# Attention between two routed FFNs on one core: score banks in pairs, three query tiles moved by squares, values later

## The reference, cut to what matters

```
q = LN(x) @ Wq.T + bq
scores = q @ memory_keys.T / sqrt(128)          # 4096 tokens x 4096 keys
probs = softmax(scores)
x = x + (probs @ memory_values) @ Wo.T + bo
```

## Time and profile before

| | us |
|---|---|
| time, median of 3 runs | 713.45 (712.92 to 713.6) |
| the profiled execution: its time | 712.66 |
| its span | 710.6 |
| TensorE busy | 644.7 |
| VectorE busy | 533.0 |
| ScalarE busy | 470.7 |
| GpSimd busy | 285.5 |
| mean granted TensorE clock (share of 2.4 GHz, no time) | 0.99 |

### The profile page before, as it was taken

The page is one execution under the profiler, slowest core; times in us unless marked ns, Lnnn a source line. Parts: engine busy times, 40 slices in busy tenths (PEclk is TensorE's granted clock), DMA queues, the critical chain, the costliest instruction groups (busy, mean ns, idle before and its releaser), DMA issues.

```text
span 710.6 us, 9499 instructions
## 1 busy us (share of the span) xinstructions
PE 644.7 (91%) x3009; PEld 453.5 (64%) x3024; DVE 533.0 (75%) x1048; ACT 470.7 (66%) x893; POOL 285.5 (40%) x354
## 2 busy tenths in 40 slices
PE   3898988769999999999999999999999989889997
PEld 2444443557777777777777776777777777645542
DVE  3799876757867787677686877767777885799885
ACT  3577887546675665766766667666666556478886
POOL 4655412043534434254252443425433547642200
PEclk9899999989999999999999999999999999999999
DMA  7011100225043150422505224051340504000001
GB/s 280 2 37 54 59 30 0 65 55 119 15 104 81 40 119 8 112 66 55 119 1 118 57 63 104 15 119 36 85 107 13 119 9 110 1 0 31 30 15 45
DMA packets 24803, 44.39 MB, mean 62 GB/s; under 512 B 4955, under 2 KB 5555, under 8 KB 24627
## 3 DMA queue, kind: packets, MB, share of 16 engines
q1 hardware_dynamic: 24467, 43.78, 24.6%
q10 hardware_dynamic: 288, 0.01, 0.0%
HBM read 8.12 MB, written 2.10 MB: 14 GB/s over the span
## 4 chain that ended last, share of the span: by engine, by line
PE 40%; DVE 31%; ACT 15%; issue 9%; POOL 2%; SPq 1%; DMA 1%; ACTq 0%; DVEq 0%; POOLq 0%
DVE bank_max L929 10%; DVE E L881 8%; DVE p_lo L874 5%; ACT E L629 4%; PE banks L1175 4%; ACT probs L639 4%; PE banks L1055 4%; PE banks L1220 4%; PE banks L1222 3%; PE banks L1221 3%; PE banks L1064 3%; PE banks L1177 3%; PE banks L1176 3%; ACT p_hi L606 3%; DVE probsT L788 3%
## 5 line engine op out<-in xcount | busy, mean ns | idle before, releaser
L418 POOL TENSOR_TENSOR p_lo<-probsT,p_hi 128x512 fp32r<-128x512 f32 x128 | 164.3, 1289 | 286.6 <-ACT p_hi L614 286.6
L929 DVE TENSOR_REDUCE bank_max<-banks 128x1 f32<-128x512 f32 (+1 forms) x192 | 162.0, 853 | 23.4 <-PE banks L1177 21.0
L874 DVE TENSOR_TENSOR p_lo<-banks,p_hi 128x512 fp32r<-128x512 f32 x128 | 87.7, 685 | 97.0 <-ACT p_hi L606 96.8
L629 ACT ACTIVATE E<-banks,neg_max 128x512 f32<-128x512 f32 (+1 forms) x96 | 79.3, 830 | 91.8 <-DVE neg_max L954 86.2
L1175 PE MATMUL banks<-kv_lo,q_parts 128*128 128x512 f32 x256 | 113.9, 445 | 27.0 <-ACT probs L639 13.4
L639 ACT ACTIVATE probs<-banks,neg_max 128x512 f32<-128x512 f32 (+1 forms) x96 | 79.3, 830 | 73.3 <-DVE neg_max L954 73.3
L509 ACT ACTIVATE probsT<-probsT 128x1024 bf16<-128x1024 bf16 x96 | 92.3, 981 | 33.0 <-DVE probsT L788 24.3
L788 DVE SCALAR_TENSOR_TENSOR probsT<-banks,E 128x1024 bf16<-128x1024 f32 x80 | 95.5, 1219 | 22.5 <-PE banks L1055 19.6
L1220 PE MATMUL banks<-p_hi,kv_lo 128*128 128x512 f32 x256 | 107.9, 421 | 1.5 <-POOL p_lo L418 1.3
L1222 PE MATMUL banks<-p_hi,kv_hi 128*128 128x512 f32 x256 | 102.3, 400 | 0.0
L1221 PE MATMUL banks<-p_lo,kv_hi 128*128 128x512 f32 x256 | 102.0, 399 | 0.0
(11 more groups left out here) (101 smaller groups left out, 867.7 us busy)
## 6 DMA issues: line engine op xcount, KB each, us to landing
probsT<-E SPq DMA_DIRECT2D x256, 128.0 KB, 2.4
kv_stage<-in_keys_values SPq DMA_DIRECT2D x8, 512.0 KB, 3.5
out<-X SPq DMA_DIRECT2D x8, 256.0 KB, 2.0
X<-in_x SPq DMA_DIRECT2D x1, 1280.0 KB, 9.2
X<-in_x SPq DMA_DIRECT2D x3, 256.0 KB, 5.3
probs<-in_wup SPq DMA_DIRECT2D x1, 704.0 KB, 5.3
probs<-in_wdown SPq DMA_DIRECT2D x1, 704.0 KB, 6.6
sup_s<-in_shared_up SPq DMA_DIRECT2D x1, 88.0 KB
```

Of the source, the lines that this page charges most:

```text
L418: pool.tensor_tensor(moved_part(p_lo, ring), moved_pair(w, m), moved_part(p_hi, ring).bitcast(fp32), ALU.subtract).then_inc(moved_lo_done, 1)
L874: dve.tensor_tensor(own_part(p_lo, ring), own_squares(ring), own_part(p_hi, ring).bitcast(fp32), ALU.subtract).then_inc(p_lo_done, 1)
L929: dve.tensor_reduce(bank_max[:, i % 2, k:k + 1], score_banks(u, i)[:, first:first + count, :].rearrange("p b n -> p (b n)"), AX.X, ALU.max ...
```

## The change: pairs of banks, a third moved tile, a later value sum

1. **Banks.** Banks 0 to 5 are three pairs (SCORE_PAIRS). Half a tile's scores (two banks, 1024 keys) fill one pair. The programs walk over **half tiles**, 8 a unit, counted through as H = 8u + h. The scores of half H wait for the exponential of half H - 3. There is one bank TB (bank 6) for all transposes and projections, and one bank OB (bank 7) for the value sums.
2. **Tiles.** MOVED = 3: tiles 0 to 2 go by squares, TensorE transposes only tile 3 (two transposes for each pair of chunks). The transfers go in two batches of 16: tiles 0 and 1 after their squares, then tile 2 after its own.
3. **Lag.** In half H TensorE transposes pair H - 12 (FILL_HALF) and sums the values of pair H - 14 (VALUE_HALF).
4. **Maxima and exponentials** are 1024 wide throughout (before: 1024, 512, 512 and 512, 512, 1024).
5. **Blocks.** Each unit's projection goes to TB, ScalarE copies it to y for both blocks, and GpSimd multiplies it by the share and adds it to X (`add_block`); VectorE no longer does it.
6. Buffers share other memory: kv_stage lies in E2's third tile, the xT copies in probs, the staged FFN weights in probsT.

The diff, cut to its core:

```diff
-EXP_PIECES = ((0, 1), (1, 1), (2, 2))
-MOVED = 2
+MOVED = 3
+OWN = GT - MOVED
+BATCHES = ((0, 2), (2, 1))
-VLAG = 4
-MAX_BANKS = ((0, 2), (2, 1), (3, 1))
+SCORE_PAIRS = 3
+HALVES = 2 * GT
+LAG = 12
+FILL_HALF = HALVES + LAG // 2 - 2
+VALUE_HALF = HALVES + LAG // 2
+PROJECT_HALF = LAG // 2 + 1
+Q_HALF = 5
...
+        def score_pair(u, i, h):
+            p = (2 * (u * GT + i) + h) % SCORE_PAIRS
+            return banks[:, 2 * p:2 * p + 2, :]
...
+        def pair_at(H, first_half):
+            return H - first_half if 0 <= H - first_half < UNITS * UP else None
...
         # sync
-                sp.wait_ge(squares_done, 2 * MOVED * (u + 1))
-                for b in range(QUADS):
-                    for i in range(QUADS):
-                        sp.dma_start(
+                for k, (first, count) in enumerate(BATCHES):
+                    sp.wait_ge(squares_done, 2 * (MOVED * u + first + count))
+                    for b in range(QUADS):
+                        for i in range(QUADS):
...
+                            sp.dma_start(target, E2[i * SQ:(i + 1) * SQ, first:first + count, b, :]
+                                         ).then_inc(moved[k], 16)
...
         # gpsimd
+            def add_block(w):
+                g, v = w // 2, w % 2
+                pool.wait_ge(y_copied, w + 1)
+                pool.wait_ge(merge_b, 4 * g + 4)
+                pool.tensor_tensor(y[:, :, :], y[:, :, :], share[:, v, :].unsqueeze(2).to_broadcast([P, GT, D]),
+                                   ALU.mult).then_inc(y_scaled, 1)
...
+                pool.tensor_tensor(X[:, tiles_of(g), :], X[:, tiles_of(g), :], y[:, :, :], ALU.add
+                                   ).then_inc(block_added, 1)
...
+                    ring = pair_at(u * HALVES + h, VALUE_HALF - 4)
+                    if ring is not None:
+                        moved_low(ring)
...
+                    if 2 <= u and h == LAG // 2:
+                        add_block(u - 2)
...
         # scalar, in each half
+                    if 2 <= u and h == LAG // 2 - 2:
+                        copy_oT(u - 2)
+                    ring = pair_at(H + 1, FILL_HALF)
+                    if ring is not None:
+                        own_high(ring)
+                    if u < UNITS:
+                        exponentials(u, h // 2, h % 2)
...
+                    ring = pair_at(H, VALUE_HALF - 4)
+                    if ring is not None:
+                        moved_high(ring)
...
         # vector, in each half
+                    ring = pair_at(H - 1, FILL_HALF)
+                    if ring is not None:
+                        own_low(ring)
+                    if u < UNITS:
+                        maximum(u, h // 2, h % 2)
+                        if h % 2 == 1:
+                            negative_maximum(u, h // 2)
...
+                    at_u, at_h = divmod(H - 2, HALVES)
+                    if 0 <= at_u < UNITS and at_h // 2 < MOVED:
+                        transpose_squares(at_u, at_h // 2, at_h % 2)
...
+                    if u == LAST + 1 and h >= 5:
+                        for k in range(6 * (h - 5), min(6 * (h - 4), STEPS + 1)):
                             route_group(k, GROUPS)
...
         # tensor, in each half
+                    if u < UNITS and H >= 2:
+                        scores(u, h // 2, h % 2)
+                    filled = max(0, min(H - FILL_HALF, UNITS * UP))
+                    if 2 <= u and h == PROJECT_HALF:
+                        wait(pe, p_lo_done, filled)
+                        project_out(u - 2)
...
+                    ring = pair_at(H, VALUE_HALF)
+                    if ring is not None:
+                        values(ring)
+                    ring = pair_at(H, FILL_HALF)
+                    if ring is not None:
...
+                        transpose_pair(ring)
```

More of the change, by code:

```diff
@@ L212, in macaron_kernel @@
         squares_done = sem("squares_done")
-        moved = sem("moved")
+        moved = [sem(f"moved{k}") for k in range(len(BATCHES))]
         p_hi_done = sem("p_hi_done")
@@ L695, in _, with own_high, moved_high @@
[L695 to L697 removed]
+            def own_high(ring):
+                act.wait_ge(probsT_done, ring + 1)
+                wait(act, pv_done, 2 * (ring - HI_RING + 1))
+                act.activation(own_part(p_hi, ring), own_squares(), ACT.Copy).then_inc(p_hi_done, 1)
+            def moved_high(ring):
+                if ring % UP == 0:
+                    for k in range(len(BATCHES)):
+                        act.wait_ge(moved[k], moves(ring // UP + 1))
+                wait(act, pv_done, 2 * (ring - HI_RING + 1))
+                act.activation(moved_part(p_hi, ring), moved_pair(ring // UP, ring % UP), ACT.Copy
+                               ).then_inc(moved_hi_done, 1)
@@ L698, in _ @@
+            copy_wbc(GROUPS, banks[:, 2, :])
             ffn(1)
@@ L1012, in shared_up_product @@
                 last.then_inc(shared_up_done, 1)
-            def early_gate(i):
-                pe.wait_ge(xT_copied, SECOND_LN + i + 1)
-                pe.wait_ge(expz_done, GROUPS + i - 1)
-                for t in range(GT):
-                    last = pe.matmul(early_logits(i)[:, t * E:(t + 1) * E], xT[i][:, t * P:(t + 1) * P], gate_s[:, :],
-                                     start=True, stop=True)
-                last.then_inc(logits_done, 1)
             def transpose_weights(G, bank):
@@ L1140, in ffn, with transpose_for_q @@
                     pe.wait_ge(kv_lo_done, KV // 2)
-                    for q in range(BANKS):
-                        scores(0, 0, 0, 0, q)
+                    scores(0, 0, 0)
+                    scores(0, 0, 1)
                 transpose_back(base + GROUPS - 1)
-            def transpose_for_q(g):
+            def transpose_for_q(g, bank):
                 pe.wait_ge(normalized, g + 1 + ATTENTION_LN)
-                wait(pe, x_attended, g - 1)
                 pe.wait_ge(wbc_copied, GROUPS - AHEAD + 1)
-                transpose_x(xT_bank)
@@ L1151, in project_q @@
-            def project_q(g):
+                transpose_x(bank)
+            def project_q(g, bank):
                 pe.wait_ge(xT_copied, g + 1 + ATTENTION_LN)
-                pe.matmul(xT_bank[:, :], wq_scaled[:, :], xq[:, :], start=True, stop=True).then_inc(q_projected, 1)
-            def scores(u, g, v, i, q):
-                slot = u * GT + i
-                last = slot - (2 if slot <= GT else 1)
-                wait(pe, exp_done, last * len(EXP_PIECES) + (1, 2, 3, 3)[q])
-                if slot == 1 and q == 0:
+                pe.matmul(bank[:, :], wq_scaled[:, :], xq[:, :], start=True, stop=True).then_inc(q_projected, 1)
@@ L1224, in project_out, with values @@
-            def project_out(u, v):
-                if u == 2:
+            def values(ring):
+                w, m = divmod(ring, UP)
+                pe.wait_ge(p_lo_done, ring + 1)
+                pe.wait_ge(moved_lo_done, ring + 1)
+                if m == 0:
+                    wait(pe, oT_copied, w)
+                    if w == 0:
+                        pe.wait_ge(kv_lo_done, KV)
+                        pe.wait_ge(q_ready, 1)
+                for half in range(2):
+                    c = 2 * m + half
+                    value = ((w % 2) * KC + c) * D
+                    vh = kv_hi[:, KV // 2 + value // KVW, value % KVW:value % KVW + D]
+                    vl = kv_lo[:, KV // 2 + value // KVW, value % KVW:value % KVW + D]
+                    hi = p_hi[:, ring % HI_RING, :, half * SQ:(half + 1) * SQ]
+                    lo = p_lo[:, ring % HI_RING, :, half * SQ:(half + 1) * SQ]
+                    pe.matmul(OB, vl, hi, start=(c == 0), stop=False)
+                    pe.matmul(OB, vh, lo, start=False, stop=False)
+                    pe.matmul(OB, vh, hi, start=False, stop=(c == KC - 1)).then_inc(pv_done, 1)
```

615 lines of the change are left out of this document (252 added, 363 removed).

## The result

The changed kernel took 695.7 us (693.85 to 697.09, 4 runs), the kernel before 713.18 in the same rounds: a ratio of 0.976, 95% interval 0.974 to 0.978. The time is inside the range, the gain is 17.5 us where 37 were forecast. The profiled execution took 697.09, its span is 695.3.

What follows compares the result with a forecast made beforehand. TensorE was taken as nearly the bound (55.3 of 60.0 us per two units). Start 159, steady part 381, end 41, second FFN 89.4 plus 2.5 gave a 672.9 span; adding 2.06 and 0.8 made 676 us, range 662 to 702.

Steps and rivals of the forecast that it cites:

- TensorE's own work: Steady attention: a half tile takes TensorE 3.085 us, two units 52.5; the profile should show 52.5 to 54.
- The transfers: Second batch lands 17.7 to 22.8 us after tile 1's squares, wanted at about 21; counted as nothing in steady state.
- Its own late case: Steady-state transfers landing at the late end: 0.4 us a unit, 6 us in all, not counted.
- Waits of 7 us in the steady part: TensorE waiting, chiefly at bank TB for VectorE's low part: 7 us in all, bounds 0 and 33.
- The start: First score at 119.35; second batch lands at 153 to 158; first half with values starts at 159 us.
- The end: From the last scores to the second FFN: 41 us, with 14 pairs of values left and uncovered.
- GpSimd paces: At the end: 12 subtractions 21.9, old work 6.1, one `add_block` 2.6, late copies 2.5; 35.5 with the starting 2.4.
- The second FFN: After the attention: 89.4 us as before, plus 2.5 because its first `transpose_x` waits for GpSimd's last `add_block`.
- The first (waits stay, 702): TensorE still waits 2.35 us a unit because TB and OB are single; 702 us, chance 0.2.
- The second (GpSimd dearer, 696): Subtractions cost GpSimd 1.93 us, nothing overlaps at the end, more VectorE instructions are blocked; 696 us, chance 0.11.
- The third: VectorE's two-SBUF-input instructions in `merge_shifts` and `merge_shares` wait out GpSimd subtractions; slower, 724 us, chance 0.05.
- a middle unit over 28 us: Sign that the prediction is wrong; the wait ahead of TensorE's projections, fills or scores then names the rival.

Runs made afterwards that it cites:

- experiment 1: From the third unit on, only 8 of the second batch's 16 transfers issued (old numbers used there), against the changed kernel: 680.62 us, ratio 0.956.
- experiment 3: Changed kernel with the same 32 transfers batched as one tile, then two, instead of two, then one: 683.65 us, ratio 0.960.
- experiment 7: On experiment 3, VectorE instead of GpSimd scales and adds the output blocks (`add_block`): 682.46 us, ratio 0.955.
- experiment 5: Changed kernel with the same bytes in three batches of one tile, 48 issues a unit instead of 32: 763.44 us, ratio 1.070.
- experiment 4: Changed kernel with four of the second batch's sixteen transfers issued by ScalarE, SP keeping 28 a unit: 685.91 us, ratio 0.963.
- experiment 6: On experiment 3, at the end a layer norm and the weight spreading one half earlier on GpSimd, weight transposition one half later on TensorE: 676.02 us.
- experiment 8: On experiment 3, the last unit's eight subtractions of moved pairs on VectorE instead of GpSimd: 669.93 us, ratio 0.939.
- experiment 12: Changed kernel with its own batches, plus the changes of experiment 6 and experiment 8 at the end: 681.69 us, ratio 0.955.
- experiment 9: Changed kernel with experiment 3, experiment 6 and experiment 8 joined: 670.99 us, ratio 0.941.
- experiment 2: Changed kernel with the first moved copy of each unit one half later in ScalarE's order: 710.29 us, ratio 0.996.
- experiment 11: On experiment 9, eight of the sixteen transfers of the first unit's second batch issued by ScalarE: 668.75 us, ratio 0.938.

## Why the prediction was half right

- **TensorE's own work: right.** Two units at 52.8 in experiments 1, 3 and 7, forecast 52.5 to 54; the changed kernel itself had 52.9 to 55.4. The six banks in pairs did what the sum said. No wait for a score bank is left in a middle unit.
- **The transfers: the step that failed in the middle.** It said "In steady state I count nothing; ScalarE's slack of 1.3 is the cover, and the late end would cost 0.4 a unit". The row of SP's issues was in the sum: 17.7 to 22.8 after tile 1's squares is the first 16 issues, then the second batch, then the landing. But the lower end was the pace of bytes and the upper end the price of an issue, and the rows had the price, 0.64. Only the upper end was possible, and it was exceeded: the second 16 issues took 10.1 in the first unit and 11.3 in the one looked at, where one took 1.77, and the batch was there at 23.2. The copy wanted it at 20.2, not at 21. So ScalarE waited 3.0; its slack of 1.3 covered what it was said to, and 1.68 reached TensorE. The mechanism and the cover were right, the term was put at nothing. Its own late case would have been 6 us; experiments 1 and 3 show it to be worth 12, and 3 and 5 that it is the issues.
- **Waits of 7 us in the steady part.** Without the late batch there are 3.5, so VectorE's low part ahead of the projections was a thin place, but a cheap one. That the steady part was only 5.5 longer than forecast, though the late batch cost 12, is luck: 3.5 of the 7 were not needed, and an undisturbed half took 3.03 (five of them from 360.69 to 375.82), not 3.085, which is 6.3 in 114 halves. Some 3 us went the other way, in the projections and preparations; I did not divide them.
- **The start: 6.0 late.** The second batch landed at 159.1 (I had 153 to 158 and took the middle); the first score was 1.2 later, at 120.5, a mark that moved by 2 us from run to run; and TensorE ran at 1.2 GHz until about 167.8. In experiment 4 a landing 2.5 earlier came with values 3.9 earlier, part of it by the clock. How the rest divides wasn't tried.
- **The end: 41 became 53.7, the largest error and the second step that failed.** The sum "GpSimd paces" had 12 subtractions, 6.1 of the old end's work and one `add_block`, 30.6 in all; GpSimd was busy for 37.3. There were 13 subtractions and two `add_block`, and the layer norms, casts and weights came to 9.2 instead of 6.1. The other half of the error was that I let the waits of an in-order GpSimd come to 2.5 in all. Experiment 6 shows 7.6 us of it to be order alone. Experiment 8 shows 13.7 to go when eight subtractions leave GpSimd, and 12, with both changes and the late batch still there, shows 14.0. The order and the load overlap (experiment 9), so how much of the end each of them is can't be divided further. About half of either gain is the clock, which the sum of the end did not have at all: in the changed kernel it was granted 0.87 there.
- **The second FFN:** 90.2, against 91.9. Its first `transpose_x` did not wait.
- **The rivals.** The first (waits stay, 702) named the right place, TB, and a cause that isn't it: experiments 1 and 3 remove the wait without touching TB. The second (GpSimd dearer, 696) gives nearly the measured time, for the wrong reason in the steady part, where GpSimd's subtraction cost 1.84 and made nobody wait, and for a partly right one at the end; that it came out so near is luck. The third's mechanism was there, in `merge_shifts`, at 2.1 us a group on VectorE, but nothing of it reached TensorE; it did in experiment 2 alone. The sum had 0.2 of waiting for `merge_shares` and nothing for `merge_shifts`, which was right for TensorE and not for VectorE. That a middle unit over 28 us would make the prediction wrong held: four of six units with a preparation were, but the wait ahead of `transpose_x` for VectorE's low part would have named the first rival, and the true cause stood two engines further back.

## What to carry to other kernels

Add up the issuing queue as an engine of its own: issues a period times the time of one, and what stands ahead in its order when the data is ready; grouping the same transfers otherwise gave 12 us here for one line. Where a measured price of an issue and a pace of bytes give two ends of a range, the slower of the two sets the time, and a wait whose upper end is over its cover isn't nothing. Before a second queue is given a part of the transfers, look at the DMA share: at 0.40 the issues set the pace and four of them moved to ScalarE helped (experiment 4), at 0.88 the engines were nearly full and eight moved ones did nothing (experiment 11). And before an instruction with two SBUF inputs on VectorE or a row of GpSimd work is moved, look at what the two will meet.

## What was new in the hardware

A transfer of 128 or 64 KB inside SBUF costs the queue that issues it 0.59 to 0.60 us, whatever its size, and the next issue starts 0.63 to 0.64 us after it began; 11 of the changed kernel's 512 took longer than 0.9, the longest 2.05. ScalarE's queue pays 0.61 for the same beside SP's when the transfers have 64 KB, and up to 1.33 when both queues issue 128 KB. And a VectorE instruction of 0.16 us lasted to within 0.03 us of the end of the GpSimd subtraction that it met, and no longer, though the next subtraction of the row was already free to start.
